# A transformer layer on one core: the first layer norm folded behind the projection, its input also loaded transposed

## What is computed

```python
x = L0_attn_x                                   # (16, 512, 128)
x = x + attention(layernorm(x))                 # 16 heads of 8, 4 key heads, window of 32
x = x + experts(layernorm(x))                   # top 2 of 8, hidden size 256

def layernorm(x, eps=1e-5):
    return (x - mean(x)) / sqrt(var(x) + eps)   # no weights of its own
def attention(h):
    q, k, v = h @ Wq.T, h @ Wk.T, h @ Wv.T      # per head of 8
    q, k = rotary(rms_norm(q)), rotary(rms_norm(k))     # rms_norm: eps 1e-6
    att = softmax(where(mask, q * q_gain @ k.T / sqrt(8), -big))
    return mix_pairs_of_heads(att @ v) @ Wo.T
```

## Time and profile before

| | us |
|---|---|
| median of 3 runs | 556.38 (552.81 to 558.29) |
| the profiled execution, its own time | 555.95 |
| its span, first to last instruction | 554.2 |
| busy in the span: PE, DVE, ACT, POOL | 479.6, 424.6, 369.7, 346.2 |

### The profile page before, as it was taken

How to read it: one execution, slowest core, us unless ns; L and a number is a source line. 1 busy time by engine, 2 the same in 40 slices (tenths; PEclk the granted TensorE clock), 3 DMA queues, 4 the chain that set the end, 5 groups by cost and what they waited for, 6 DMA issues and landing times. The chain is left out here.

```text
span 554.2 us, 25600 instructions
## 1 busy us (share of the span) xinstructions
PE 479.6 (87%) x8607; PEld 423.0 (76%) x8607; DVE 424.6 (77%) x1698; ACT 369.7 (67%) x1170; POOL 346.2 (62%) x536
## 2 busy tenths in 40 slices
PE   3898888999898999899785988997999999999940
PEld 1477777777676777778674888996999999999940
DVE  5788898999999899999998456645666666667662
ACT  4466777777777677778554786674777777777720
POOL 3333225678777687778756658363666666667765
PEclk9999999999999899999897699899999999999985
DMA  7333333344332222222232133344565555564642
GB/s 229 68 74 85 86 73 83 75 112 99 87 75 56 72 62 55 55 59 60 57 89 80 61 107 112 88 128 130 160 168 154 163 155 158 161 163 137 171 126 72
DMA packets 126319, 58.21 MB, mean 105 GB/s; under 512 B 54000, under 2 KB 121712, under 8 KB 126192
## 3 DMA queue, kind: packets, MB, share of 16 engines
q1 hardware_dynamic: 117424, 38.89, 28.3%
q0 software_dynamic: 8192, 16.79, 10.6%
q10 hardware_dynamic: 576, 0.88, 0.5%
HBM read 28.01 MB, written 24.58 MB: 95 GB/s over the span
## 5 line engine op out<-in xcount | busy, mean ns | idle before, releaser
L1288 POOL DMA_INDIRECT expert_in<-xn,slot_r x128 | 127.1, 993 | 69.9 <-DVE slot_r L912 44.7
L1359 POOL DMA_INDIRECT ga<-expert_out,row_all x128 | 122.0, 953 | 74.8 <-DVE yb L1248 32.7
L721 PE MATMUL chb<-xbT,wcur 128*128 128x128 f32 x1144 | 155.8, 281 | 0.0
L721 PEld LDWEIGHTS chb<-xbT,wcur 128*128 128x128 f32 x1144 | 143.6, 197 | 0.0
L417 ACT ACTIVATE pT<-chb 128x512 f32<-128x512 f32 x128 | 76.7, 599 | 70.9 <-PE chb L633 47.1
L1241 DVE TENSOR_TENSOR hT<-sil,chb 128x256 f32<-128x256 f32 x143 | 60.2, 421 | 81.0 <-ACT sil L507 78.8
L524 ACT COPY wcur<-wgu 128x512 f32 x143 | 90.0, 629 | 6.3 <-issue 5.9
L507 ACT ACTIVATE sil<-chb 128x256 f32<-128x256 f32 x143 | 54.9, 384 | 56.5 <-PE chb L721 50.0
L929 DVE TENSOR_REDUCE mx<-chb 128x8 f32<-128x512 f32 x128 | 85.9, 679 | 4.1 <-PE chb L633 3.7
L580 PEld LDWEIGHTS pv<-vext,pT 128*32 128x32 f32 x3968 | 45.1, 110 | 24.3 <-issue 18.4
L580 PE MATMUL pv<-vext,pT 128*32 128x36 f32 x3968 | 54.1, 202 | 11.0 <-issue 8.4
(11 more groups left out here) (140 smaller groups left out, 1018.6 us busy)
## 6 DMA issues: line engine op xcount, KB each, us to landing
xb<-expert_in SPq DMA_DIRECT2D x143, 64.0 KB, 2.3
expert_out<-yb SPq DMA_DIRECT2D x71, 128.0 KB
xa<-x SPq DMA_DIRECT2D x16, 256.0 KB, 3.5
out<-oo SPq DMA_DIRECT2D x31, 128.0 KB, 2.0
qk<-qk SPq DMA_DIRECT2D x64, 48.0 KB, 1.8
wgu<-w_gu SPq DMA_DIRECT2D x16, 128.0 KB
expert_in<-xn,slot_r POOLq DMA_INDIRECT x128
ga<-expert_out,row_all POOLq DMA_INDIRECT x128
```

The costliest lines, as they stand in the source:

```text
L721: last = nc.tensor.matmul(chb[:, b % 4, n * P:(n + 1) * P], wcur[:, b % 3, n * P:(n + 1) * P], xbT[:, b % 4, :], start=True, stop=True)
L1288: nc.gpsimd.indirect_dma_start(xs_dram, bass.IndirectOffsetOnAxis(ap=slot_r[:, q % 4, 2 * v + k:2 * v + k + 1], axis=0), xn2[:, t % 16, :] ...
L1359: nc.gpsimd.indirect_dma_start(ga[:, q % 2 * TPS + v, j, :], None, ys_dram[0:min(blocks, LIVE) * P, :], bass.IndirectOffsetOnAxis(ap=row_a ...
```

## The change

The projection is linear, so the norm can be applied behind it. The mean is removed by the weights: wp becomes (I - 1/128) times the given weights (centre, one matmul before step 0, copied by ACT). The projection then reads x transposed, which SP loads a second time from an input laid out that way (xT, one transfer of 256 KB a group), so xh, its transpose and its third of the batch copy go. The deviation is left out of the queries and keys, whose rms norm cancels it, if the rms norm's eps is scaled by the variance (eb1, a bias of lnr for each token, made by DVE); the values are multiplied by rs1 as ACT copies them. The statistics are taken by ACT: an Identity scaled by -1/128 whose accumulator gives less_mean, and a Square with less_mean as bias whose accumulator gives spread; the elements themselves are written to a scratch tile. bn_stats, bn_aggr and the shift of the first norm go from DVE. The projection moves ahead of TensorE's wait for the batch copy.

```diff
@@ loads (SP and ACT)
-        for_proj = ((ident, ident_in), (wp, w_proj))
+        for_proj = ((centre, centre_in), (wpr, w_proj), (ident, ident_in))
+            def load_xT(q):
+                sp.dma_start(xTs[:, q % 2, :], xT[:, q * SEQ:(q + 1) * SEQ]).then_inc(xT_in[q % 2], 16)
                 if q is not None and q + 4 < SEQS:
-                    sp.wait_ge(ln1_stats, (TPS + 1) * (q + 1))
+                    sp.wait_ge(spread_ok, TPS * (q + 1))
                     load_x(q + 4)
+                q = group(s, L_XT + 1)
+                if q is not None and q + 2 < SEQS:
+                    sp.wait_ge(proj_done, (q + 1) * TPS)
+                    load_xT(q + 2)
             load_x(0)
+            load_xT(0)
             load_x(1)
+            load_xT(1)
@@ ACT
+            act.wait_ge(centred, 1)
+            nc.scalar.copy(wp[:, :], pp[:, 0:PF]).then_inc(wp_ok, 1)
-                live = [n for n, lag in enumerate((L_XT, L_TY, L_TX2)) if tile(s, lag) is not None]
+                live = [n for n, lag in ((1, L_TY), (2, L_TX2)) if tile(s, lag) is not None]
...
                     nc.scalar.copy(xyT[:, s % 2, now], tp[:, now]).then_inc(xyT_ok, 1)
+                t = tile(s, 0)
+                if t is not None:
+                    q, v = t // TPS, t % TPS
+                    act.wait_ge(x_in[q % 4], (q // 4 + 1) * 16)
+                    nc.scalar.activation(unused[:, 0, :], xa[:, t, :], ACT.Identity, scale=-1.0 / DIM,
+                                         accum_out=less_mean[:, q % 2, v:v + 1]).then_inc(mean_ok, 1)
...
                     act.wait_ge(ss_ok, t + 1)
-                    nc.scalar.activation(lnr[:, r, :], ss[:, r, :], ACT.Ln, bias=HD * RMS_EPS).then_inc(act_ln, 1)
-                t = tile(s, L_XH)
+                    act.wait_ge(eb1_ok, q + 1)
+                    nc.scalar.activation(lnr[:, r, :], ss[:, r, :], ACT.Ln, bias=eb1[:, q % 2, v:v + 1])\
+                      .then_inc(act_ln, 1)
+                t = tile(s, 0)
                 if t is not None:
-                    act.wait_ge(nb1_ok, q + 1)
-                    wait(act, batch_done, batches(t - 4 + L_XT))
-                    nc.scalar.activation(xh[:, t % 4, :], xa[:, t, :], ACT.Identity, scale=rs1[:, q % 2, v:v + 1],
-                                         bias=nb1[:, q % 2, v:v + 1]).then_inc(xh_ok, 1)
+                    act.wait_ge(mean_ok, t + 1)
+                    nc.scalar.activation(unused[:, 1, :], xa[:, t, :], ACT.Square, bias=less_mean[:, q % 2, v:v + 1],
+                                         accum_out=spread[:, q % 2, v:v + 1]).then_inc(spread_ok, 1)
...
-                    nc.scalar.copy(vtok[:, t % 8, :], pp[:, 2 * HF:PF]).then_inc(v_ok, 1)
+                    act.wait_ge(rstd1, 2 * (q + 1))
+                    nc.scalar.activation(vtok[:, t % 8, :], pp[:, 2 * HF:PF], ACT.Identity,
+                                         scale=rs1[:, q % 2, v:v + 1]).then_inc(v_ok, 1)
@@ TensorE
+            nc.tensor.matmul(pp[:, 0:PF], centre[:, :], wpr[:, :], start=True, stop=True).then_inc(centred, 1)
-                if tx is not None:
-                    pe.wait_ge(xh_ok, tx + 1)
-                    last = nc.tensor.transpose(tp[:, 0:P], xh[:, tx % 4, :], ident[:, :])
+                t = tile(s, L_XT)
+                if t is not None:
+                    q, v = t // TPS, t % TPS
+                    if v == 0:
+                        pe.wait_ge(xT_in[q % 2], (q // 2 + 1) * 16)
+                    wait(pe, t12_ok, t)
+                    wait(pe, v_ok, t)
+                    nc.tensor.matmul(pp[:, 0:PF], xTs[:, q % 2, v * P:(v + 1) * P], wp[:, :], start=True, stop=True)\
+                      .then_inc(proj_done, 1)
                 if batches(s) > batches(s - 1):
                     pe.wait_ge(xyT_ok, batches(s))
-                t = tile(s, L_XT)
-                if t is not None:
-                    wait(pe, t12_ok, t)
-                    nc.tensor.matmul(pp[:, 0:PF], xyT[:, s % 2, 0:P], wp[:, :], start=True, stop=True)\
-                      .then_inc(proj_done, 1)
@@ DVE
+            def scaled_eps(q):
+                dve.wait_ge(spread_ok, TPS * (q + 1))
+                wait(dve, act_ln, (q - 1) * TPS)
+                nc.vector.tensor_scalar(eb1[:, par, :], spread[:, par, :], HD * RMS_EPS / DIM, HD * RMS_EPS * LN_EPS,
+                                        ALU.mult, ALU.add).then_inc(eb1_ok, 1)
-                    shift(q, mv1, rs1, nb1, rstd1, nb1_ok)
+                    scaled_eps(q)
-                t = tile(s, 0)
-                if t is not None:
-                    nc.vector.bn_stats(st1[:, t % TPS, :], xa[:, t, :]).then_inc(ln1_stats, 1)
-                q = group(s, 0)
-                if q is not None:
-                    aggregate(q, st1, mv1, ln1_stats)
```

More of the change, by code:

```diff
@@ L83, in batches @@
 def batches(s):
-    return min(max(s - L_XT + 1, 0), NT + L_TX2 - L_XT)
+    return min(max(s - L_TY + 1, 0), NT + L_TX2 - L_TY)
 def scores(s):
@@ L134, in run, with kernel_body @@
     return link
-def kernel_body(nc, x, w_proj, rope, gain, wo_self, wo_pair, mix_self, mix_pair, w_router,
-                w_gu, w_dn, ident_in, eyes_in, masks_in, selg_in, tri_in, region_in, cells_in, out):
+def kernel_body(nc, x, xT, w_proj, rope, gain, wo_self, wo_pair, mix_self, mix_pair, w_router,
+                w_gu, w_dn, ident_in, eyes_in, masks_in, selg_in, centre_in, tri_in, region_in, cells_in, out):
     xs_dram = nc.dram_tensor("expert_in", (BASE * P, DIM), F32, kind="Internal").ap()
@@ L170, in kernel_body @@
         xa = sb("xa", [P, NT, DIM])
-        st1, mv1 = sb("st1", [P, TPS, 6]), sb("mv1", [P, 2, TPS, 2])
-        ln1, rs1, nb1 = sb("ln1", [P, 2, TPS]), sb("rs1", [P, 2, TPS]), sb("nb1", [P, 2, TPS])
+        less_mean, spread, unused = sb("less_mean", [P, 2, TPS]), sb("spread", [P, 2, TPS]), sb("unused", [P, 2, DIM])
+        ln1, rs1, eb1 = sb("ln1", [P, 2, TPS]), sb("rs1", [P, 2, TPS]), sb("eb1", [P, 2, TPS])
         st2, mv2 = sb("st2", [P, TPS, 6]), sb("mv2", [P, 2, TPS, 2])
         ln2, rs2, nb2 = sb("ln2", [P, 2, TPS]), sb("rs2", [P, 2, TPS]), sb("nb2", [P, 2, TPS])
-        xh, xyT = sb("xh", [P, 4, DIM]), sb("xyT", [P, 2, TX])
+        xTs, xyT = sb("xTs", [P, 2, SEQ]), sb("xyT", [P, 2, TX])
         sq, ss = sb("sq", [P, 4, RF]), sb("ss", [P, 4, RF // HD])
@@ L235, in kernel_body @@
         rec_ok, acc_ok = sem("rec_ok"), sem("acc_ok")
-        ln1_stats, rstd1, nb1_ok, act_ln = sem("ln1_stats"), sem("rstd1"), sem("nb1_ok"), sem("act_ln")
+        mean_ok, spread_ok, rstd1, eb1_ok, act_ln = sem("mean_ok"), sem("spread_ok"), sem("rstd1"), sem("eb1_ok"), sem("act_ln")
         ln2_stats, rstd2, nb2_ok = sem("ln2_stats"), sem("rstd2"), sem("nb2_ok")
-        xh_ok, batch_done, xyT_ok, proj_done = sem("xh_ok"), sem("batch_done"), sem("xyT_ok"), sem("proj_done")
+        centred, wp_ok = sem("centred"), sem("wp_ok")
+        xT_in = [sem(f"xT_in{n}") for n in range(2)]
+        batch_done, xyT_ok, proj_done = sem("batch_done"), sem("xyT_ok"), sem("proj_done")
         v_ok, t12_ok, ss_ok, rms_ok = sem("v_ok"), sem("t12_ok"), sem("ss_ok"), sem("rms_ok")
@@ L406, in _, with rstd @@
             act.preload_act_table_set("natural_log_exp_and_others")
-            def rstd(q, mv, ln, rs, stats, done):
+            act.wait_ge(centred, 1)
+            nc.scalar.copy(wp[:, :], pp[:, 0:PF]).then_inc(wp_ok, 1)
+            def rstd(q, variance, scale, ln, rs, done):
                 par = q % 2
-                act.wait_ge(stats, (TPS + 1) * (q + 1))
-                nc.scalar.activation(ln[:, par, :], mv[:, par, :, 1], ACT.Ln, bias=LN_EPS).then_inc(done, 1)
+                nc.scalar.activation(ln[:, par, :], variance, ACT.Ln, scale=scale, bias=LN_EPS).then_inc(done, 1)
                 act.wait_ge(done, 2 * q + 1)
@@ L481, in step @@
                 if q is not None:
-                    rstd(q, mv1, ln1, rs1, ln1_stats, rstd1)
+                    act.wait_ge(spread_ok, TPS * (q + 1))
+                    rstd(q, spread[:, q % 2, :], 1.0 / DIM, ln1, rs1, rstd1)
                 q = group(s, L_TY + 1)
                 if q is not None:
-                    rstd(q, mv2, ln2, rs2, ln2_stats, rstd2)
+                    act.wait_ge(ln2_stats, (TPS + 1) * (q + 1))
+                    rstd(q, mv2[:, q % 2, :, 1], 1.0, ln2, rs2, rstd2)
             def route(s):
@@ L543, in _ @@
             pe.wait_ge(c_proj, len(for_proj) * 16)
+            nc.tensor.matmul(pp[:, 0:PF], centre[:, :], wpr[:, :], start=True, stop=True).then_inc(centred, 1)
             def transposes(s, turned):
-                tx, ty, t2 = tile(s, L_XT), tile(s, L_TY), tile(s, L_TX2)
+                ty, t2 = tile(s, L_TY), tile(s, L_TX2)
                 last = None
@@ L677, in products @@
                     pe.wait_ge(max_ok, 2 * t + 2)
+                    wait(pe, stm_ok, t)
                     nc.tensor.transpose(tp[:, TX:TX + P], mx[:, t % 4, :, :].rearrange("p c n -> p (c n)"),
@@ L690, in _ @@
```

(10 more changed lines are left out.)

15 lines of the change are left out of this document (7 added, 8 removed).

## The result

| | before | after |
|---|---|---|
| median of 20 runs each | 555.6 (552.81 to 561.41) | 558.57 (555.52 to 564.09) |
| the profiled execution, its own time | 555.95 | 558.54 |
| its span | 554.2 | 556.7 |
| busy in the span: PE, DVE, ACT, POOL | 479.6, 424.6, 369.7, 346.2 | 473.1, 409.8, 390.8, 345.2 |

The ratio of after to before is 1.0068, 95% interval 1.0045 to 1.009: 2.5 to 5.0 us slower, less than the 1% beyond which the prediction called a difference measurable, and inside its range. Every ratio here leaves out the executions that took over 1.5% longer than the fastest of their kernel. VectorE was relieved of 14.8 us and the kernel became a little slower.

The account below looks back on a forecast made before the run. The prediction took a ring through ACT and DVE as the early bound, with DVE fuller later; +3.0 + 0.9 - 3.1 = +0.8 on 555.95 gave 556.8, about 557 for a median, range 546 to 565.

Parts of the forecast that it names:

- likeliest case: Whole kernel: the forecast of a near balance, about 557 us, spanning 551 to 562; chance 0.50.
- the beginning: Before the first Square of a projection: seven means and squares on ACT cost +3.4, 0.4 returns, +3.0 us.
- steps 10 to 27: Early attention steps, 4.5 groups: the ring through ACT and DVE costs +0.20 a group, +0.9 us.
- steps 28 to 63: Late attention steps, 9 groups: DVE gives back 0.80 a group, 0.46 returns as waiting, -3.1 us.
- What leaves DVE: DVE, attention steps: bn_stats 0.20 a tile, 0.80 a group; bn_aggr's 0.30 later turns into waiting for POOL.
- What is added to ACT: ACT, exp to vtok: pointer operands, the Square in place of xh and its read-out lengthen the chain by 0.24.
- a: Cost of reading out ACT's accumulator: taken as 0.11 us, with 0 and 0.30 kept as alternatives.
- d: Growth of ACT's chain from exp to vtok in each step: a + 0.13 = 0.24 us.
- the early ring: Up to step 27: maxima on DVE, exp to vtok on ACT, t12 to residual on DVE, then next maxima.
- ACT has room: Rival, attention stage: read-out and pointers hide, DVE's work sets every step; 548.5, down to 541; chance 0.26.
- The read-out is dear: Rival, ACT's accumulators: slower from a = 0.18 on; 562.3 at 0.20, up to 569; chance 0.17.
- xT collides with the keys: Rival, xT loads against the shifted keys: 1.44 for each of 8 groups, 11.5, so 568; chance 0.07.

Follow-up runs that it names:

- late_lag2_pool: After with the statistics' Square at the end of ACT's step, statistics two steps later, POOL's scatters behind tq: 549.84, ratio to before 0.9857; measured again 551.51, 0.9931.
- accum_only: Before with only ACT's accumulators replacing bn_stats and bn_aggr; xh, its transpose and the given weights stay: 559.0 us, ratio to before 1.0081.
- late_square: After with the Square of the statistics moved from between lnr and rr to the end of ACT's step, behind stm: 555.18 us, ratio to before 1.0019.
- pool_after: After with POOL reordered so that both scatters stand behind tq: 555.4 us, ratio to before 1.0001.
- fold_only: After without the accumulators: norm folded behind the projection, statistics still by DVE's bn_stats and bn_aggr: 554.88 us, ratio to before 0.9996.
- pool_before: Before with only POOL reordered so that both scatters stand behind tq: 548.4 us, ratio to before 0.9912.

## Why the prediction came out as it did

**The verdict was right.** 558.57 lies 1.6 above the 557.0, inside the range and the likeliest case's own 551 to 562; slower by 0.68% is inside the 1%. Against the kernel before in the same runs it is +3.0 by medians and +3.8 by the ratio, where the sum said +0.8. The profiled pair differs by +2.6 (558.54 less 555.95); the runs say that this pair was on the mild side. Of that pair, against the sum: the beginning +0.7, steps 10 to 27 -0.5, steps 28 to 63 +0.8, the steps behind them +1.0, the rest -0.2, together the 1.8 by which +2.6 exceeds +0.8. The two executions of late_lag2_pool differ by 0.1 in the beginning, but by 3.7 between steps 9 and 27 and by 2.5 between 27 and 63, so that these two parts came so near is partly luck.

**What leaves DVE: right.** The prediction gave 0.80 a group; the rows of steps 28 to 60 show 0.78 for bn_stats and 0.31 for bn_aggr. The change took another 0.42 from the two operations that POOL had stretched, which the prediction had not seen: 0.22 from L819, which now seldom meets tq, and 0.20 from the shift, of which one of two a group is gone. It gave back about 0.6: 0.10 in scaled_eps, the rest in small growth of many instructions, so 0.90 net (16.54 to 15.64). One of these, 0.09, is another operation beside POOL. Without bn_stats ahead of it, the router's ms (L864) starts 0.06 behind an addition of POOL and takes 0.34 or 0.35 in every late group of after; before, in this step, it started 0.25 behind and took 0.18 (the first two rows are of after, the others of before):

```profile
200.66 0.35 POOL L1329 TENSOR_TENSOR t<-t 128x80 f32<-128x80 f32 x1
200.72 0.35 DVE L864 SCALAR_TENSOR_TENSOR ms<-oh,lg 128x32 f32<-128x32 f32 x1
...
214.69 0.36 POOL L1299 TENSOR_TENSOR t<-t 128x80 f32<-128x80 f32 x1
...
214.94 0.18 DVE L831 SCALAR_TENSOR_TENSOR ms<-oh,lg 128x32 f32<-128x32 f32 x1
```

**What is added to ACT: right, slightly high.** a was taken as 0.11 and measures 0.09; d was 0.24 and measures 0.19. The Trainium skill, ScalarE: Activation LUTs, What ACT_TABLE_LOAD costs, gives a fixed time, a time a column and some 93 ns for each pointer operand; an estimate from its figures is 0.293 for 128 columns without pointer operands and 0.386 with one. The trace agrees (0.29 to 0.31 and 0.39 to 0.40). The read-out comes on top. The forecast that the early ring would neither gain nor lose much stands: t12 directly behind vtok, steps of 3.66 to 3.73 against 3.74, a shift of +3.70 at step 9 and +4.07 at step 27, so +0.4 where +0.9 was said, a difference well inside that between two executions at step 27.

**The beginning: a term mis-sized by 0.7.** +3.0 was said, +3.70 measured at step 9. The work was right to 0.01 (0.82 a tile); it began 0.38 late (6.83, said 6.45), since the centring matmul waited for its load until 5.57, and the 0.4 that was to come back was 0.13 (+3.83 at step 6 to +3.70).

**Steps 28 to 63: the sum near, the waits others than said.** -3.1 was said, the shift went from +4.07 to +1.78, -2.3. The prediction let 0.46 a group come back, nearly all as waits for vtok: t12 directly behind vtok in two or three steps of a group. It is so (0.04 or less) in 13 of the 32 steps from 28 to 59, between one and two of a group, and the waits for vtok that the list shows are 0.13 a group. What came back most is the wait for POOL's tq, from 0.17 to 0.56 a group, more than bn_aggr's 0.30; waits for TensorE's results grew by 0.14. In the step shown the wait for tq is 0.62, not "near 0.4", because the 0.24 that POOL's tq had added to L819 turned into waiting too, as far as the small additions leave it: the step's length there is fixed at 2.63 from the slot numbers.

**What the sum did not hold.** Between steps 63 and 69 the shift rises again, +1.78 to +2.74; at step 64 TensorE waits 1.45 us for the shifted keys. Such waits fall in other steps in other executions, of the kernel before too, so no single one is explained here.

**The rivals.** *ACT has room* fell: 91% on DVE and no gain. The figure of 541 by occupancy fell with it; accum_only took 0.83 a group from DVE and its groups kept their length. *The read-out is dear* fell, 0.09. *xT collides with the keys* fell: over 25 to 280 us TensorE's wait for the shifted keys is 7.5 us in 9 times, before 7.2 in 9.

**Where the reading was too simple.** The prediction treated the kernel as a ring through ACT and DVE. The experiments show three limits within a few tenths of each other in a group: that ring, POOL's chain from the slot numbers to tq, and TensorE's results. Taking one away moved DVE's idle time to another, which fits that late_square and pool_after gave no more than 0.49 and 0.67%; it is argued from single traces, and no run takes away TensorE's limit.

## What to carry to other kernels

Price work moved to another engine by its place in that engine's order, not by the engine's share: the same Square lengthens the chain from exp to vtok by 0.24 a step between lnr and rr (1.65 against 1.41) and not at all behind stm (1.41, and 1.42 in fold_only, which has no Square of the statistics). The rest of the 0.40 that it takes stood in a wait that was there anyway. Before moving work off a full engine, look for instructions on it that take much longer in some steps than in others, and see what the neighbour is doing then: reordering one POOL wait gave 0.9%, moving 14.8 us of DVE's work gained nothing. When a wait disappears from the list and the group's length stays, look for where the same idle time is listed now.

## What was not expected of the hardware

Two DVE instructions with two inputs in SBUF, L819 and the shift nb, took 0.30 to 0.38 us instead of 0.14 in 13 places of the kernel before between 120 and 280 us; all of them started 0.07 to 0.18 after POOL's 128x128 multiply and ended 0.02 to 0.07 behind its end. Beside a scatter most took 0.13 to 0.18 (three took 0.27 to 0.46), and in pool_before those that started 0.28 or more after the multiply took 0.14 to 0.15. That an instruction's own duration hides a wait for a neighbour was in no list of waits. The accumulator's read-out is a row of its own, 0.19 us long, that costs 0.09 to the next start.
